# A new order of the calls on all five engines of a four-layer transformer kernel

## The reference, cut to what matters

```python
xm = _ln(x) * (1.0 + sc_sa) + sh_sa
q, k, v = heads(xm @ qkv_w + qkv_b)              # self-attention, 16 heads
x = x + g_sa * (attend(q, k, v) @ sa_proj_w + sa_proj_b)
xn = _ln(x)
q = heads(xn @ q_w + q_b)                        # cross-attention, 77 keys
k, v = heads(context @ kv_w + kv_b)
x = x + attend(q, k, v) @ ca_proj_w + ca_proj_b
xm = _ln(x) * (1.0 + sc_ff) + sh_ff
h = gelu(xm @ fc1_w + fc1_b)
x = x + g_ff * (h @ fc2_w + fc2_b)
# layer 3: x = x + mha(xn, xn, xn); x = x + mha(x, u, u); x = x + ffn(ada_ln(x))
```

## Time and profile before

| what | value |
|---|---|
| median of 3 executions | 2887.1 us (2883.17 to 2896.83) |
| the profiled execution's own time | 2888.95 us |
| its span on the core | 2887.1 us |
| mean granted TensorE clock | 0.974 of full |
| PE busy | 2716.0 us (94%), 24276 matmuls |
| DVE / ACT / POOL busy | 1834.0 us (64%) / 1554.4 us (54%) / 949.1 us (33%) |
| DMA queue q1 (SP's) | 259.65 MB, 36.7% of 16 engines |
| chain that ended last | PE 58%, DVE 6%, issue 5%, POOL 2%, DMA 2%, SP's queue 2% |

### The profile page before, as it was taken

How to read it: one execution, slowest core, us unless ns; L and a number is a source line. 1 busy time by engine, 2 the same in 40 slices (tenths; PEclk the granted TensorE clock), 3 DMA queues, 4 the chain that set the end, 5 groups by cost and what they waited for, 6 DMA issues and landing times.

```text
span 2887.1 us, 64022 instructions
## 1 busy us (share of the span) xinstructions
PE 2716.0 (94%) x24276; PEld 2292.3 (79%) x24276; DVE 1834.0 (64%) x3776; ACT 1554.4 (54%) x2715; POOL 949.1 (33%) x963
## 2 busy tenths in 40 slices
PE   7999999994899999999999999999999999999998
PEld 6999999993577777777777777777777778778776
DVE  2444444434667777777677777777676676776753
ACT  3444444432365656655555566556555665665653
POOL 3444444321123333333232332332333223333223
PEclk9999999996799999999999999999999999999998
DMA  5123222105244453454455544434445445445331
GB/s 158 63 93 102 90 82 91 51 9 159 66 101 98 102 120 91 101 115 104 121 121 134 115 92 109 117 88 108 120 108 145 117 105 115 92 103 109 90 79 42
DMA packets 280418, 290.63 MB, mean 101 GB/s; under 512 B 90736, under 2 KB 206816, under 8 KB 280112
## 3 DMA queue, kind: packets, MB, share of 16 engines
q1 hardware_dynamic: 268656, 259.65, 36.7%
q10 hardware_dynamic: 11456, 26.88, 3.0%
HBM read 105.33 MB, written 35.85 MB: 49 GB/s over the span
## 4 chain that ended last, share of the span: by engine, by line
PE 58%; DVE 6%; issue 5%; POOL 2%; DMA 2%; SPq 2%; ACT 1%; ACTq 0%; POOLq 0%; DVEq 0%
PE gbank L3394 9%; PE obank L3234 8%; PE obank L3241 6%; PE gbank L3234 6%; PE obank L3319 5%; PE score L3299 4%; PE obank L3365 3%; PE score L3285 3%; DVE m_a L2596 2%; PE score L3348 2%; PE gbank L3249 2%; PE gbank L3334 2%; PE obank L3334 2%; PE gbank L3225 2%; PE obank L3468 1%
## 5 line engine op out<-in xcount | busy, mean ns | idle before, releaser
L2049 ACT ACTIVATE p_f<-score 128x1024 f32<-128x1024 f32 (+1 forms) x576 | 566.9, 1022 | 243.2 <-PE score L3299 219.3
L2596 DVE TENSOR_REDUCE m_a<-score 128x4 f32<-128x1024 f32 x384 | 459.4, 1218 | 132.6 <-PE score L3285 132.3
L1897 POOL TENSOR_TENSOR h_c<-h_f,h_c 128x512 fp32r<-128x512 f32 x192 | 246.4, 1284 | 640.5 <-DVE h_c L2670 640.5
L3394 PE MATMUL gbank<-w_down,h_c 128*128 128x256 f32 x2304 | 336.5, 294 | 1.2 <-POOL h_c L1897 1.2
L3394 PEld LDWEIGHTS gbank<-w_down,h_c 128*128 128x128 f32 x2304 | 292.4, 190 | 16.0 <-POOL h_c L1897 1.6
L1153 PE MATMUL m_ps<-m_comb,m_w 128*128 128x256 f32 x2304 | 295.4, 284 | 1.5 <-PEq L253 1.5
L1153 PEld LDWEIGHTS m_ps<-m_comb,m_w 128*128 128x128 f32 x2304 | 279.9, 188 | 5.0 <-issue 3.6
L2606 DVE TENSOR_REDUCE m_b<-gbank 128x4 f32<-128x308 f32 x192 | 92.1, 480 | 224.5 <-PE gbank L3334 191.7
L768 POOL TENSOR_TENSOR m_hhl<-m_hf,m_hhl 128x512 fp32r<-128x512 f32 x96 | 125.1, 1303 | 267.2 <-DVE m_hhl L992 267.2
L3319 PE MATMUL obank<-p_f,v_s 128*20 128x256 f32 x3072 | 204.2, 396 | 0.5 <-ACT p_f L2049 0.4
L3299 PE MATMUL score<-q_cat,k_cat 50*128 50x256 f32 x1536 | 190.3, 318 | 9.7 <-DMA q_cat<-mT_a 7.9
(11 more groups left out here) (289 smaller groups left out, 5613.6 us busy)
## 6 DMA issues: line engine op xcount, KB each, us to landing
q_cat<-q_hl SPq DMA_DIRECT2D x288, 128.0 KB, 3.5
k_cat<-k_hl SPq DMA_DIRECT2D x288, 128.0 KB, 3.8
qc_cat<-qc_hl SPq DMA_DIRECT2D x288, 128.0 KB, 3.1
split_L<-m_cut SPq DMA_DIRECT2D x36, 512.0 KB, 4.1
x_a<-x_after_L SPq DMA_DIRECT2D x48, 256.0 KB, 2.6
x_b<-x_after_L SPq DMA_DIRECT2D x48, 256.0 KB, 4.2
kc_cat<-kc_hl SPq DMA_DIRECT2D x288, 39.0 KB, 2.0
x_after_L<-y_c SPq DMA_DIRECT2D x32, 256.0 KB, 2.4
```

What stands on the lines that cost most here:

```text
L1897: e.tensor_tensor(h_c[:, 1, 2 * i:2 * i + 2, :], h_f[:, i % 2, :, :], h_c[:, 0, 2 * i:2 * i + 2, :].bitcast(F32), ALU.subtract).then_inc(S ...
L2049: e.activation(p_f[i % 4][0:n, :], score[i % 2].ap[0:n, :, :].rearrange("p h n -> p (h n)"), ACT.Exp, scale=SCALE).then_inc(ex.sem, 1)
L2596: e.tensor_reduce(m_a[:, :, i::NPAIR].rearrange("p t h -> p h t"), score[i % 2].ap[:, :, :].rearrange("p h (t k) -> p h t k", t=TT), AX.X, ...
L3394: mm = e.matmul(B_DOWN.ap[:, tt, :], h_c[:, xp, 2 * i + c, tt * P:(tt + 1) * P], W["down"][:, i, wp, c, :], start=(i + wp + xp + c == 0), ...
```

## The change

The set of calls is the same (only calls that fetch nothing are fewer, and no helper is changed): each engine's list is in a new order, in the fill, in the steady loop and in the drain. The whole diff is 3625 lines, because the fill and drain are written out; the steady period is given here, with s for the unit in `self_scores`, "-" for a call's old place and "+" for its new one.

```diff
# TensorE (L3719)
...
 self_scores(s, 1)
-cross_projected(s-2)
 down(s-3, 0)
...
 down(s-3, 2)
+cross_projected(s-2)
 down(s-3, 3)
-self_values(s, 0)
 self_scores(s, 2)
...
 cross_plain(s-1, 0, 1)
-down(s-3, 4)
+self_values(s, 0)
 self_scores(s, 4)
...
 cross_plain(s-1, 1, 1)
+self_values(s, 1)
 self_scores(s, 5)
-self_values(s, 1)
 cross_plain(s-1, 2, 0)
 cross_plain(s-1, 2, 1)
+down(s-3, 4)
 self_scores(s, 6)
+cross_plain(s-1, 3, 0)
+cross_plain(s-1, 3, 1)
+self_scores(s, 7)
 down(s-3, 5)
-cross_plain(s-1, 3, 0)
-self_scores(s, 7)
-cross_plain(s-1, 3, 1)
 down(s-3, 6)
+down(s-3, 7)
 cross_max_rows(s-1)
-down(s-3, 7)
 self_plain(s+1, 0)
 self_plain(s+1, 1)
+mlp_turned(s-2)
 self_values(s, 2)
 self_values(s, 3)
-mlp_turned(s-2)
-values(s+1, 0)
 cross_scores(s-1, 0)
 cross_scores(s-1, 1)
+values(s+1, 0)
 values(s+1, 1)
-context_turned(s)
 cross_scores(s-1, 2)
...
 up(s-2, 0)
+context_turned(s)
 self_plain(s+1, 3)
# VectorE (L2985)
...
 self_x_low(s+1)
+context_stats(s)
 self_max_low(s)
 cross_x_low(s-1)
-context_stats(s)
+mlp_h_high(s-3, 2)
+cross_queries_low(s-1)
+keys_low(s+1)
 mlp_h_high(s-3, 3)
 cross_heads_normed(s-2)
-keys_low(s+1)
-cross_queries_low(s-1)
+self_stats(s+2)
+queries_low(s+1)
+context_normed(s)
 cross_sum(s-2)
-queries_low(s+1)
-mlp_stats(s-2)
 cross_max(s-1, 0, 0)
 cross_max(s-1, 0, 1)
-context_normed(s)
 cross_max(s-1, 1, 0)
 cross_max(s-1, 1, 1)
-mlp_normed(s-2)
+mlp_stats(s-2)
 cross_max(s-1, 2, 0)
...
 cross_max(s-1, 3, 1)
-self_stats(s+2)
+mlp_normed(s-2)
+self_normed(s+2)
+mlp_gated(s-3)
 cross_max_low(s-1)
-mlp_gated(s-3)
-self_normed(s+2)
 self_max(s+1, 0)
...
 mlp_x_high(s-2)
+values_out(s+1)
 mlp_x_low(s-2)
-values_out(s+1)
 self_recips(s)
...
 self_max(s+1, 5)
+self_heads_normed(s)
+cross_recips(s-1)
+self_max(s+1, 6)
+cross_keys_low(s)
+cross_values_out(s)
 mlp_h_high(s-2, 1)
-self_heads_normed(s)
-self_max(s+1, 6)
-cross_recips(s-1)
-cross_keys_low(s)
 self_sum(s)
-cross_values_out(s)
 cross_stats(s)
 self_max(s+1, 7)
-mlp_h_high(s-2, 2)
 cross_normed(s)
# ScalarE (L2374)
...
 cross_queries_high(s-1)
-exp_table(s-3)
 queries_high(s+1)
...
 self_weights(s, 5)
-self_heads(s, 0)
 self_weights(s, 6)
...
 cross_max_high(s-1)
+exp_table(s-1)
+mlp_modulated(s-2)
+self_heads(s, 0)
 self_heads(s, 1)
-mlp_modulated(s-2)
 cross_weights(s-1, 0)
...
 gelu_table(s-2)
+cross_heads(s-1, 1)
 context_out(s)
-cross_heads(s-1, 1)
 mlp_act(s-2, 0)
# GpSimd (L1949)
...
 self_rstd(s+1)
+mlp_rstd(s-3)
+cross_residual(s-2)
 mlp_sum(s-4)
...
 mlp_h_low(s-3, 1)
+cross_rstd(s-1)
+context_rstd(s)
+mlp_h_low(s-3, 2)
+mlp_h_low(s-3, 3)
 self_out_gated(s)
 mlp_residual(s-3)
-cross_rstd(s-1)
-mlp_h_low(s-3, 2)
-mlp_h_low(s-3, 3)
-cross_residual(s-1)
-context_rstd(s)
-mlp_rstd(s-2)
# SyncE (L1657)
...
 load_x(s+2)
+max_out_a(s, 1)
+max_out_a(s, 0)
+cross_key_rows_low(s-1)
 cross_query_rows_high(s-1)
...
 query_rows_high(s+1)
-query_rows_low(s+1)
 key_rows_high(s+1)
 key_rows_low(s+1)
+query_rows_low(s+1)
 load_residual(s)
...
 sums_out_a(s)
+recips_out_a(s)
 pack_a(s)
-recips_out_a(s)
 sums_out_b(s-1)
+load_context(s+1)
+store(s-3)
+recips_out_b(s-1)
 load_self_gate(s+1)
 pack_b(s-1)
-store(s-3)
 cross_key_rows_high(s)
-recips_out_b(s-1)
-load_context(s+1)
-cross_key_rows_low(s)
-max_out_a(s+1, 0)
-max_out_a(s+1, 1)
```

The fill, at the point where the first units start (SP's and ACT's lists hold most of it):

```diff
@@ SyncE @@
             load_x(0)
-            load_self_gate(0)
-            load_residual(0)
-            load_mlp_bias(0)
-            load_context(0)
-            load_mlp_gate(0)
             load_x(1)
             query_rows_high(0)
@@ ScalarE @@
             queries_high(1)
+            first_of_the_rest()
             self_max_high(0)
-            first_of_the_rest()
@@ VectorE @@
+            self_stats(1)
             values_out(0)
-            queries_low(0)
...
             keys_low(0)
-            self_stats(1)
...
+            queries_low(0)
```

More of the change, by code:

```diff
@@ new lines, in _ @@
+            down(1, 6)
+            cross_max_rows(3)
+            down(1, 7)
+            self_values(4, 2)
+            self_plain(5, 0)
+            self_plain(5, 1)
+            mlp_turned(2)
+            self_values(4, 3)
+            cross_scores(3, 0)
+            values(5, 0)
+            context_turned(4)
+            cross_scores(3, 1)
+            cross_scores(3, 2)
+            values(5, 1)
+            cross_values(3, 0)
+            cross_values(3, 1)
+            cross_scores(3, 3)
@@ new lines, in _ @@
+            self_scores(5, 5)
+            cross_plain(4, 1, 1)
+            self_values(5, 1)
+            cross_plain(4, 2, 0)
+            self_scores(5, 6)
+            cross_plain(4, 2, 1)
+            down(2, 4)
+            cross_plain(4, 3, 0)
+            self_scores(5, 7)
+            cross_plain(4, 3, 1)
+            down(2, 5)
+            down(2, 6)
+            down(2, 7)
+            cross_max_rows(4)
+            self_plain(6, 0)
+            self_plain(6, 1)
+            mlp_turned(3)
@@ new lines, in _ @@
+            self_scores(6, 6)
+            down(3, 4)
+            down(3, 5)
+            down(3, 6)
+            cross_plain(5, 3, 0)
+            cross_plain(5, 3, 1)
+            self_scores(6, 7)
+            down(3, 7)
+            cross_max_rows(5)
+            self_plain(7, 0)
+            self_values(6, 2)
+            self_plain(7, 1)
+            mlp_turned(4)
+            self_values(6, 3)
+            cross_scores(5, 0)
+            values(7, 0)
+            values(7, 1)
+            cross_scores(5, 1)
@@ new lines, in _ @@
+            self_scores(41, 6)
+            cross_plain(40, 2, 1)
+            down(38, 4)
+            down(38, 5)
+            cross_plain(40, 3, 0)
+            cross_plain(40, 3, 1)
+            self_scores(41, 7)
+            down(38, 6)
+            cross_max_rows(40)
+            down(38, 7)
+            self_plain(42, 0)
+            self_plain(42, 1)
+            mlp_turned(39)
+            self_values(41, 2)
+            self_values(41, 3)
+            cross_scores(40, 0)
+            cross_scores(40, 1)
@@ new lines, in _ @@
+            self_scores(42, 7)
+            cross_plain(41, 3, 0)
+            cross_plain(41, 3, 1)
+            down(39, 6)
+            down(39, 7)
+            cross_max_rows(41)
+            self_plain(43, 0)
+            self_plain(43, 1)
+            mlp_turned(40)
+            self_values(42, 2)
+            self_values(42, 3)
+            cross_scores(41, 0)
+            cross_scores(41, 1)
+            values(43, 0)
+            values(43, 1)
+            cross_scores(41, 2)
+            cross_values(41, 0)
```

2523 lines of the change are left out of this document (1998 added, 525 removed).

## The result

| kernel | median us | range | against the kernel before, 95% interval |
|---|---|---|---|
| before | 2891.97 | 2883.17 to 2897.07, 4 executions | |
| changed | 2850.01 | 2846.95 to 2866.16, 4 executions | 0.9869, 0.9822 to 0.9917 |
| changed, a second set | 2840.98 | 2833.45 to 2854.83, 4 executions | 0.9831, 0.9792 to 0.9869 |

The forecast was 2853, a gain of 34.6 us. Measured are 42 in the first set and 48 in the second, both clear of the noise. The size came out; the reasons did not, and that is what the rest is about. The profiled execution of the changed kernel was its slowest, 2866.16 (span 2864.4).

The account below looks back on a forecast made before the run. TensorE was taken to set the pace, busy 42.09 of 43.70 us per period. Gains of 16.0 + 3.0 + 10.6 + 5 = 34.6 us gave 2853 us against the median, range 2840 to 2868.

Parts of the forecast that it names:

- Step 1: Turn of xn_b: GpSimd's `cross_rstd` ahead of `self_out_gated` starts xn_b about 0.55 us sooner, 29 times, 16.0 us.
- Step 2: Long wait at 1547.02 behind gate_a's DMA goes, 3.0 us; some 1.7 us of half speed estimated behind it.
- Steps 3 and 4: TensorE's `down` regrouped, VectorE's `self_stats` ahead of the cross reductions: 0.26 us per period, 41 periods, 10.6 us.
- Step 3: `down` in three groups, `self_values(0)` moved out ahead of the cross scores: TensorE's sequence up to `self_plain(0)` 0.3 us shorter.
- rival A: Only the turn of xn_b gains; savings up to `self_plain(0)` are waited away, fill gives nothing: about 2870 us, chance 0.20.
- its two points: `self_plain(0)` and the second `cross_scores`, where TensorE was said to idle 0.95 us per period.
- Step 5: ScalarE's exp table load moves behind q's high half; exponentials start 0.95 us later, hidden behind the downs, no cost.
- Step 6: `cross_residual` behind `mlp_rstd` on GpSimd delays SP's `max_out` of mT_b, landing just in time: no cost, thin margin.
- Rival C: Late `cross_residual` holds SP's `load_residual` and `max_out`, so the first cross score waits every period, 37 us: 2900, chance 0.08.
- Rival B: SP's packed queue lands rows 0.5 us later, costing 20 and leaving some 10 of 34.6: 2878 us, chance 0.17.
- Step 7: Fill: earlier `self_stats(1)` and mT_a evacuation shorten the waits at 680.86 and 705.87, 5 us, bounds -5 and 12.

Follow-up runs that it names:

- experiment 1: Kernel before with one line moved on GpSimd, `cross_rstd` ahead of `self_out_gated` and `mlp_residual`: 2965.77 us, 1.026 of the kernel before.
- (5): Kernel before with one line moved on VectorE, `mlp_h_high` 2 behind `cross_x_low` instead of ahead of `cross_normed`: 2863.37 us, 0.9892 of the kernel before.
- experiment 10: Kernel before with only TensorE's calls from `self_scores(0)` to `self_plain(0)` in the new order: 2900.14 us, 1.0026 of the kernel before.
- (6): Kernel before with one line moved on VectorE, `self_normed` ahead of `mlp_gated`: 2886.88 us, 0.9974 of the kernel before.
- experiment 12: Changed kernel with `mlp_gated` ahead of `self_normed` again on VectorE: 2884.71 us, 0.9957 of the kernel before.
- experiment 3: Changed kernel with one line moved on GpSimd, `self_out_gated` right behind `cross_rstd`: 2869.27 us, 0.9923 of the kernel before.
- experiment 8: Changed kernel with ScalarE's weight loads for the next layer moved and spread among later calls: 2828.87 us, 0.9788 of the kernel before.

## Why the prediction was right and where it was wrong

*Step 1 (16.0 us)* failed in its reason. It said that GpSimd's order makes the wait and that `cross_rstd` ahead of `self_out_gated` cures it. The wait went and gave 1.06 us a period, twice the 0.55 and more than the 0.71 that the step had as its bound. But alone that move costs 77 us (experiment 1), and without it, by one cast moved on VectorE, 29 us are won (5). The step in that working that failed is the bound "the next bound for xn_b is VectorE's reduction": it took the operation's 1.69 for its cost, where half of it was time behind GpSimd. The `mlp_h_high` that the change took from in front of `cross_normed`, and that the prediction names without a price, mattered because it released `mlp_h_low`. The bound was too low because the row of waits shows less than there was to win: from the turn of the maxima to that of xn_b it was 1.04 us, of which the row calls 0.67 a wait, and is 0.22 now, and the products behind come 0.2 closer as well.
The Trainium skill, "SBUF — State Buffer", "SBUF: two separate sides", says that GpSimd and VectorE, when it runs in a mode that uses both its ports or reads two inputs from SBUF, share a pair of ports under an exclusive lock, held for a whole instruction by whoever starts first. The rows agree: in experiment 10, where VectorE's pair of x_a operations got in first, they took 0.72 together and GpSimd's `mlp_sum` beside them 1.70 in place of 1.38. In which mode these operations run, no run here shows. I hadn't weighed this page, and should have: it would have given a larger gain for steps 1 and 4.

*Step 2 (3.0 us)* failed. The 2.70 us for gate_a at 1547 is gone, but the period around 1500 took 53.8 us in the profile after and 54.9 in the second, against 47.3: the weight loads had moved too. The prediction followed the calls of ScalarE that compute and left out `next_up_low` and `next_up_high`, whose issues are part of a moved step. Its 1.7 us of half speed isn't in the two rows that it names, which differ by 0.4; the profile has the granted clock at half for 3.4 us from 1547.1.

*Steps 3 and 4 (10.6 us)* were put at half of what came: 0.26 a period against 0.54 in layers 1 and 2. Step 3's own term failed. It had TensorE's own time up to `self_plain(0)` shorter by 0.3; without its waits that time goes from 15.30 to 15.15, and in experiment 10, with the same new stretch, to 15.31. It wasn't waited away, as rival A had it: the waits in this stretch are 0.43 us a period before and 0.42 after. Now they stand at `cross_plain` (14.3 us in 22 times, 0.65 each, within the bound of 0.7) and at `self_plain(0)`, for the q rows (7.4 in 17), together just over the 0.4 a period that the prediction had set as its sign against step 3. One reason for the missing half is in the list of calls: `cross_projected` stands between `down(2)` and `down(3)`, so `down` runs in four groups (0 to 2, 3, 4, 5 to 7) and not in the three that I had counted, one group fewer and not two. The 0.95 us that the prediction has idle at its two points is 0.43 and 0.22 in these averages. The gain came behind `self_plain(0)`, from VectorE's chain, of which the collision on x_a was the part that I had not seen. Freed alone it gave 5 us (6); what it is worth in the new order isn't shown, since experiment 12 moves a wait together with it.

*Step 5* held: no wait for an exponential stands at `self_values`, and the score tiles wait 1.9 us for them in two places, 1.6 in two before. The drain of 1.38 us that the prediction cites beside the load doesn't show in the trace before: the load of 1.28 at 1194.17 starts 0.02 behind the operation ahead of it, and the next starts at 1195.46, 0.01 behind its end. *Step 6* held, with the thin margin it named: 4.0 us in three waits, against 2.8 in two before. Rival C's mechanism, priced at 37 us, is real: experiment 12 runs into the same wait for 39.5 by delaying another link of that chain. Rival B's sum is off: 34.6 less 20 leaves 14.6 and not 10, so 2872. *Step 7* (5 us) was right in size and half right in its reason: unit 8 starts 4.1 us sooner (1063.1 to 1059.0), 7.3 in the second profile. The turn of x_a waits 2.41 in place of 5.05, as expected, but the wait for mT_a behind it is 8.00 in place of 4.98.

Together, for the two profiles: 43 and 45 us of shorter periods and 4 and 7 of the fill, less 23 and 9 that more half clock took back and 2 in the pipeline's drain; that is the 23 and 41 us by which the spans are shorter. The forecast had 29.6 for the periods, some 14 too few, and nothing for the clock. Two errors of opposite sign cancel, so that the number is this close is luck.

## What to carry to other kernels

When the same VectorE operation on the same shape has two durations in a trace (here 400 and 1334 ns), look for a large GpSimd operation that started ahead of it before explaining the wait by order; moving the one that *releases* the GpSimd work can be the whole fix. A reordering moves DMA issues with it: list the bulk loads and where they go out against the small transfers that the next matmul waits for. An order on one engine can't be judged alone: TensorE's part of this change gained nothing by itself, and the move on GpSimd that looked like its core cost 77 us.

## What the runs showed of the hardware

- Two engines on SBUF: a TENSOR_SCALAR of 128x256 took 400 ns alone and 1334 beside a GpSimd operation of 128x512 that had started first; a cast of 128x512 0.42 and 1.55. All of it counts as VectorE's busy time. Not every operation is held up: in the kernel before, the TENSOR_REDUCE of m_a from PSUM took 1215 ns in the 204 cases that started beside such an operation and 1222 alone, a BATCH_NORM_STATS2 413 and 418.
- Small DMAs beside bulk loads of another queue: q rows of 128 KB landed 3.8 us after their issue in a period without loads, 7.0 beside two w_up pieces of 512 KB.
- A wait of 1.2 to 3 us on TensorE can cost more than itself: behind it the granted clock was 0.50 for 3.4 to 17.1 us (the longest in experiment 3), and calls that take 7.5 us at full clock took 13.6. It doesn't always follow: a wait of 2.6 us at 2231 in the kernel before and five of 1.0 to 2.0 in experiment 8 had none, and at 2203 and 2296 in the changed one half clock came with no wait above 0.9 just ahead.
